# Loading the third dense stage's weights ahead of the query stores of the last layer

## The chip, the cores and the metric

The kernel runs on one core of one Trainium2 chip. The core has a matrix engine (PE, with its weight loads shown as PEld), a vector engine (DVE), an activation engine (ACT), a general engine (POOL) and SyncE (SP), which here only issues transfers. Transfers issued by SP and by POOL are carried out by the same 16 DMA engines. The metric is the time of one execution on the device in microseconds; lower is better. The instruction streams are written out by hand, and the engines meet only at semaphores.

## The reference

Four layers work on 8 sequences of 256 tokens with 256 features (2048 tokens). Each layer adds a gated cross-attention to a context and then a gated feed-forward stage. Cut to what matters:

```python
x = x + tanh(g_xattn[l]) * xattn_l(layernorm(x), ctx)   # 16 heads of 16
x = x + tanh(g_ffn[l]) * ffn_l(layernorm(x))
# ffn_0: light and heavy dense stage; ffn_1, ffn_2: 8 experts, top 2; ffn_3: ternary weights
def weight_quant(w):
    scale = 1.0 / clip(mean(abs(w)), 1e-05)
    return clip(round(w * scale), -1, 1) / scale
# ffn_3: h = bit_linear(x, w1); depthwise conv; silu; bit_linear(h, w2)
```

The weights of `ffn_3` are two matrices of 1024 x 256 floats, 1 MB each. `weight_quant` needs the mean absolute value of each whole matrix before any of it can be rounded.

## The kernel before

Attention keeps its operands as a high and a low part, each stored to memory and loaded again in a stacked form. For each of four groups of 512 tokens (g = 0 to 3), PE projects keys and values from the context, then queries from the normed and transposed x. ACT writes the high part (`keys` L1292, `queries` L1334), DVE the low part (`keys_low` L1764, `queries` L1774). SP stores both parts of a group to `qk_parts` in two transfers of 512 KB (`store_k` L397, `store_q` L404). POOL loads the stacks back for each sequence b (`load_stack` L547, rows of 1 KB), keys first, then queries, and waits for the stored group before each. A group's query parts sit in one of two buffers, so the high part of group 2 waits for the store of group 0, and that of group 3 for the store of group 1. The scores of the attention begin (`scores_nat` L849) when the low parts of all four groups are done and the stack of sequence 0 has landed.

The preceding stage, the experts of layer 2, ends with POOL gathering expert results by index from memory (L732, 32 transfers of 128 KB into `wslot`), and DVE adding them to `x_res` (L2150, four adds for each pair of token tiles, counted by `y_done[2]`). Between these adds DVE makes the low key parts of layer 3, so the projections of layer 3 start while the experts' results are still being added.

The ternary weights also go into `wslot`, into places that the first 24 adds have freed; hence the wait for `y_done[2]` at 24 in `load_ternary` (L411). Its two transfers, L414 (1 MB in rows of 4 KB) and L416 (1 MB in rows of 1 KB), count on `w0_in`. DVE sums the absolute values in `ternary_sums` (L1926, two reductions, L1928 and L1929), which it reaches after the low query part of group 1 and before those of groups 2 and 3. The rounding itself (L1909 to L1914) comes after the attention.

In layer 3, SP's stream is: the key stores of groups 0 to 3, the query stores of groups 0 and 1, the two weight loads, the query stores of groups 2 and 3, and nothing more until the output. SP takes them in this order and waits at each for its semaphores. Layer 2 has the same code for projections and stores without the ternary load; there POOL loads the first two experts (four transfers of 512 KB, L541 and L544) just ahead of its stack loads.

Of the kernel before, what the change touches and what calls it, by code (L numbers as in the profile page):

```python
# [95 lines left out]
def build(nc, io, upto=8):  # L96

    ctx = ExitStack()
    with ctx:
# [284 lines left out]
        @block.sync  # L384
        def _(sp):
            def load_ctx(g):
                sp.dma_start(ctx_at(g), io["ctxT"][:, g * 512:(g + 1) * 512].rearrange("(c p) t -> p c t", p=P)
                             ).then_inc(ctx_in[g], 16)
            for g in range(GROUPS):
                sp.dma_start(x_res[:, 4 * g:4 * g + 4, :],  # L390
                             io["x"][g * 512:(g + 1) * 512, :].rearrange("(t p) d -> p t d", p=P)).then_inc(x_in[g], 16)
                if g == 0:
                    sp.dma_start(ident[:], io["ident"]).then_inc(const_in, 16)
                    sp.dma_start(cols[:], io["cols"]).then_inc(const_in, 16)
                load_ctx(g)

            def store_k(l, g):  # L397

                sp.wait_ge(khi_done, GROUPS * l + g + 1)
                sp.wait_ge(klo_done, GROUPS * l + g + 1)  # L400
                for r, part in enumerate((k_hi(g), k_lo(g))):
                    sp.dma_start(rows_of(1, r, g), part.bitcast(F32)).then_inc(k_out[g % 2], 16)

            def store_q(l, g):  # L404

                sp.wait_ge(qhi_done, GROUPS * l + g + 1)
                sp.wait_ge(qlo_done, GROUPS * l + g + 1)
                for r, part in enumerate((q_hi(g), q_lo(g))):
                    sp.dma_start(rows_of(0, r, g), part.bitcast(F32)).then_inc(q_out[g % 2], 16)

            def load_ternary():  # L411

                sp.wait_ge(y_done[2], 24)
                sp.dma_start(wslot[:, 0, 0:2048].rearrange("p (c h) -> p c h", c=KC),  # L414
                             io["W1_3"].rearrange("(c p) h -> p c h", p=P)).then_inc(w0_in, 16)
                sp.dma_start(wslot[:, 1, 0:2048].rearrange("p (j d) -> p j d", d=D),  # L416
                             io["W2_3"].rearrange("(j p) d -> p j d", p=P)).then_inc(w0_in, 16)

            def load_proj(l):

                sp.wait_ge(xo_done[l - 1], B)
                sp.dma_start(wproj[:], io[f"wproj_{l}"].rearrange("w (c p) n -> p w c n", p=P)
                             ).then_inc(wproj_in, 16)
                sp.dma_start(bob[:], io[f"bo_{l}"]).then_inc(wproj_in, 16)

            for l in lo_l:
                if l in (1, 2):
                    if l == 2:
                        sp.wait_ge(lg_mm, GROUPS)
                    sp.dma_start(wg[:], io[f"wg_{l}"].rearrange("(c p) e -> p c e", p=P)).then_inc(wg_in, 16)  # L430
                if l == 0:

                    def load_mask(b):
                        for m, name in enumerate(("mask", "maskT")):
                            sp.dma_start(stage_i[:, b % 2, m].rearrange("p (a n) -> p a n", a=2),
                                         io[name][b * S:(b + 1) * S, :].rearrange("(a p) n -> p a n", p=P)
                                         ).then_inc(mask_in[b % 2], 16)
                    for b in range(2):
                        load_mask(b)
                if l == 0:  # L440
                    for g in range(GROUPS):
                        store_k(0, g)
                        store_q(0, g)
                        if g == 1:
                            sp.dma_start(v_in, io["ctx"].rearrange("(t p) d -> p t d", p=P)).then_inc(v0_in, 16)
                elif l == 1:
                    for g in range(GROUPS):
                        store_k(l, g)
                    for g in range(GROUPS):
                        store_q(l, g)  # L450
                else:
                    for g in range(GROUPS):
                        store_k(l, g)
                    for g in range(GROUPS):
                        if l == 3 and g == 2:
                            load_ternary()
                        store_q(l, g)
                if l == 0:
                    sp.dma_start(ys[2 * T:], io["ctx"][0:NT * P - 2 * T, :]).then_inc(later_in, 16)
                    sp.dma_start(tri[:], io["tri"]).then_inc(later_in, 16)  # L460
                    sp.dma_start(iotas[:], io["iotas"]).then_inc(later_in, 16)
                if l == 0:
                    for b in range(2, B):
                        sp.wait_ge(mask_done, b - 1)
                        load_mask(b)
                if l == 0:
                    sp.wait_ge(v_done, GROUPS)
                    sp.dma_start(wslots[:, 0:KC * NJ[0] * P].rearrange("p (c h) -> p c h", c=KC),
                                 io["W1_0"].rearrange("(c p) h -> p c h", p=P)).then_inc(w0_in, 16)
                    sp.wait_ge(sc_mm, 2 * PAIRS)  # L470
                    sp.dma_start(wslots[:, KC * NJ[0] * P:W0].rearrange("p (j d) -> p j d", d=D),
                                 io["W2_0"].rearrange("(j p) d -> p j d", p=P)).then_inc(w0_in, 16)
                if not ffn(l):
                    continue

                if l == 0:
                    sp.wait_ge(xo_done[0], B)
                    sp.dma_start(b2b[:], io["b2_0"]).then_inc(later_in, 16)
                    for g in range(GROUPS):
                        load_ctx(g)  # L480
                    load_proj(1)
                if l in (1, 2):
                    sp.wait_ge(xo_done[l], B)

                    for g in range(GROUPS):
                        sp.wait_ge(xn_ready, GROUPS * (2 * l + 1) + g + 1)
                        sp.dma_start(xt[g * 512:(g + 1) * 512, :].rearrange("(t p) d -> p t d", p=P), xn_slot(2 * l + 1, g)
                                     ).then_inc(xt_out, 16)
                    n0 = NT * (l - 1)

                    def load_tile(i, p):

                        sp.wait_ge(xg_mm, n0 + i - AHEAD + 1 if i < AHEAD + 2 else n0 + i - 1)
                        sp.dma_start(xg[:, p], home(i)).then_inc(xg_in[p], 16)

                    def store_tile(i, p):
                        sp.wait_ge(yo_done, n0 + i + 1)
                        sp.dma_start(ys[P * i:P * (i + 1), :], yo[:, p]).then_inc(ys_out[p], 16)
                    for i in range(AHEAD - 3):
                        store_tile(i, i % 2)  # L500
                    for i in range(AHEAD, NT):
                        if i in LATE:
                            n = LATE.index(i)
                            sp.wait_ge(late_in[n], 16 * (LATE[n + 1] - i) * l)
                        load_tile(i, i % 2)
                        if 0 <= i - 2 * AHEAD - 2 < GROUPS:
                            load_ctx(i - 2 * AHEAD - 2)
                        store_tile(i - 3, (i - 3) % 2)
                    load_proj(l + 1)
                    for i in range(NT - 3, NT):  # L510
                        store_tile(i, i % 2)

            if upto == 8:
                for g in range(GROUPS):
                    sp.wait_ge(y_done[3], 4 * (g + 1))
                    sp.dma_start(io["out"].rearrange("(t p) d -> p t d", p=P)[:, 4 * g:4 * g + 4, :],
                                 x_res[:, 4 * g:4 * g + 4, :]).then_inc(out_done, 16)
                sp.wait_ge(out_done, 16 * GROUPS)
            else:
                if upto % 2:  # L520
                    sp.wait_ge(xo_done[upto // 2], OUT[upto // 2])
                else:
                    sp.wait_ge(*ln_ready(upto // 2, upto))
                sp.dma_start(io["out"].rearrange("(t p) d -> p t d", p=P), x_res[:]).then_inc(out_done, 16)
                sp.wait_ge(out_done, 16)
# [1859 lines left out]
```

## Time and profile before

| | us |
|---|---|
| median of 3 runs | 1684.87 (1681.97 to 1688.16) |
| the profiled execution, its time | 1685.63 |
| its span in the trace | 1683.8 |
| busy: PE / DVE / ACT / POOL | 1358.9 / 999.3 / 825.0 / 652.9 |
| moved by DMA | 189.22 MB, 112 GB/s on average |

The span is what the trace covers; the profiled execution's own time is 1.83 us longer. Busy time is the time in which an engine executed instructions; a stretch in which every engine waits for a transfer does not show in it. The views used below are the chain of waits (the chain of work that ended last, followed back), the sums of waits by pair, the instructions in order of time, the issues of transfers with the time from issue to landing, and tables of stretches.

### The profile page before, as it was taken

To read this page: it belongs to the slowest core of one execution; us is meant where nothing else is said; L and a number is where in the kernel's file an instruction comes from. 1 tells how busy PE (TensorE), PEld (TensorE's weight loads), DVE (VectorE), ACT (ScalarE), POOL (GpSimd) and SP (SyncE) were. 2 spreads that over 40 slices of the span, in tenths; PEclk is the share of its full clock that TensorE was granted. 3 is DMA by queue.
4 is the path that set the end of the run, shared out by engine and by line. 5 is a ranking of instruction groups with operands and counts; after the bars stand their busy time and mean duration, and the time that the engine had idled before them with its cause. 6 is when DMAs were issued, how large, how long until landed. Compare 5 with 4: busy or idle time off the path is not lost.

```text
span 1683.8 us, 30045 instructions
## 1 busy us (share of the span) xinstructions
PE 1358.9 (81%) x9618; PEld 967.2 (57%) x9619; DVE 999.3 (59%) x2324; ACT 825.0 (49%) x1656; POOL 652.9 (39%) x711
## 2 busy tenths in 40 slices
PE   1399959998899659999998599658999837995875
PEld 1155528974565449999985355426777515564333
DVE  7266664342786753433336488684444628868787
ACT  2055545433588425555444388425555425872422
POOL 5363242011551058465216473008761626531000
PEclk9999978999799869999999799968999977997987
DMA  8997320028991325344125996114652597910001
GB/s 267 257 178 88 50 85 1 1 98 196 159 131 24 132 75 155 114 153 168 37 86 177 249 120 86 45 57 123 194 186 94 177 186 137 133 22 0 1 13 38
DMA packets 143757, 189.22 MB, mean 112 GB/s; under 512 B 21808, under 2 KB 110256, under 8 KB 143600
## 3 DMA queue, kind: packets, MB, share of 16 engines
q0 software_dynamic: 79264, 103.35, 33.8%
q1 hardware_dynamic: 64384, 84.41, 15.5%
q8 instruction: 68, 1.11, 0.3%
q14 instruction: 41, 0.34, 0.1%
HBM read 128.96 MB, written 50.99 MB: 107 GB/s over the span
## 4 chain that ended last, share of the span: by engine, by line
PE 59%; DVE 18%; DMA 9%; issue 4%; POOL 4%; ACT 4%; SPq 2%; ACTq 0%; DVEq 0%; POOLq 0%
PE PS L1073 10%; PE PS L1093 10%; PE PS L927 6%; PE PS L867 6%; PE PS L902 3%; PE PS L1085 3%; DMA stack<-mt 3%; DVE nm L1829 3%; PE PS L877 2%; DVE amx L2256 2%; DMA wslot<-ys_sorted,pos 2%; PE PS L910 2%; PE PS L964 1%; DVE xng L1713 1%; DMA wslot<-W_dram 1%
## 5 line engine op out<-in xcount | busy, mean ns | idle before, releaser
L1829 DVE TENSOR_REDUCE nm<-PS 128x2 f32<-128x512 f32 x512 | 336.4, 681 | 128.3 <-PE PS L867 51.6
L867 PE MATMUL PS<-stack 48*128 48x256 f32 x1024 | 141.0, 357 | 78.6 <-DVE nm L1829 26.2
L1093 PE MATMUL PS<-weights,hh 128*128 x936 | 187.5, 290 | 3.7 <-DVE hl L2108 3.5
L583 POOL DMA_DIRECT2D stack<-mt x128 | 71.3, 557 | 282.6 <-ACT mt L1402 280.3
L867 PEld LDWEIGHTS PS<-stack 48*128 48x128 f32 x1024 | 84.8, 204 | 164.0 <-DVE nm L1829 72.2
L1073 PE MATMUL PS<-weights,xh 128*128 x468 | 168.4, 414 | 11.8 <-ACT PS L1496 7.3
L1393 ACT ACTIVATE probs<-PS 128x512 f32<-128x512 f32 x256 | 139.0, 595 | 58.6 <-PE PS L910 31.0
L1393 ACT ACTIVATE xng<-PS 128x512 f32<-128x512 f32 x256 | 138.9, 595 | 46.9 <-PE PS L910 28.3
L1093 PEld LDWEIGHTS PS<-weights,hh 128*128 128x128 f32 x936 | 150.8, 191 | 7.7 <-issue 6.4
L1093 PE MATMUL PS<-weights,hl 128*128 x468 | 132.4, 283 | 0.0
L1506 ACT ACTIVATE hh<-PS 128x512 fp32r<-128x512 f32 x117 | 65.7, 596 | 134.5 <-PE PS L1085 134.5
L902 PE MATMUL PS<-stack 49*128 49x256 f32 x1024 | 113.3, 299 | 8.0 <-DMA stack<-mt 5.1
L1073 PEld LDWEIGHTS PS<-weights,xh 128*128 128x128 f32 x468 | 89.4, 191 | 38.2 <-issue 20.7
L1496 ACT ACTIVATE PS<-bb 128x512 f32 x117 | 67.2, 596 | 63.3 <-issue 61.6
L753 PE MATMUL PS<-ident,xng 128*128 128x128 f32 x192 | 34.5, 344 | 77.4 <-DVE xng L1713 58.8
L902 PEld LDWEIGHTS PS<-stack 49*128 49x128 f32 x1024 | 84.4, 196 | 18.2 <-issue 10.2
L1073 PE MATMUL PS<-weights,xl 128*128 x234 | 92.8, 396 | 0.0
L562 POOL DMA_DIRECT2D stack<-qk_parts x128 | 68.4, 534 | 58.7 <-DMA qk_parts<-q_parts 45.0
L1093 PEld LDWEIGHTS PS<-weights,hl 128*128 128x128 f32 x468 | 89.7, 192 | 0.0
L681 POOL TENSOR_TENSOR weights<-weights,zero 128x4096 fp32r<-128x4096 f32 (+1 forms) x12 | 63.8, 5315 | 50.5 <-DMA weights<-W_dram 50.4
L684 POOL TENSOR_TENSOR weights<-weights 128x4096 fp32r<-128x4096 f32 (+1 forms) x12 | 81.8, 6820 | 1.0
L2108 DVE TENSOR_TENSOR hl<-PS,hh 128x512 fp32r<-128x512 f32 x117 | 76.8, 684 | 6.3 <-ACT hh L1506 6.1
(298 smaller groups left out, 3039.9 us busy)
## 6 DMA issues: line engine op xcount, KB each, us to landing
stack<-qk_parts POOLq DMA_DIRECT2D x128, 256.0 KB, 4.3
qk_parts<-stack SPq DMA_DIRECT2D x32, 512.0 KB, 4.6
qk_parts<-q_parts SPq DMA_DIRECT2D x32, 512.0 KB, 6.9
stack<-qk_parts POOLq DMA_DIRECT2D x128, 128.0 KB, 3.7
weights<-W_dram POOLq DMA_DIRECT2D x12, 1024.0 KB, 7.7
ys_sorted<-yo SPq DMA_DIRECT2D x78, 128.0 KB
wide<-ctxT_dram SPq DMA_DIRECT2D x16, 512.0 KB, 7.6
weights<-W_dram POOLq DMA_DIRECT2D x12, 512.0 KB, 5.3
```

Source lines behind the costliest of these rows:

```text
L562: nc.gpsimd.dma_start(rows(first, 1), part[0:DH]).then_inc(stack_in[b % SLOTS], 16)
L583: nc.gpsimd.dma_start(stack[MAXROW:MAXROW + 65:64, b % SLOTS, 0, c:c + 2, :].rearrange("p c n -> p (c n)"), mt[:, j % 4, :]).then_inc(row_ ...
L684: nc.gpsimd.tensor_tensor(wl, w, wh.bitcast(F32), ALU.subtract).then_inc(split_done, 1)
L867: mm = pe.matmul(PS[:, (2 * t + h) % 3, qt * S:(qt + 1) * S], q[rows, qt * P:(qt + 1) * P], kk[rows], start=(l > 0 or qt == 0), stop=(l > ...
L902: mm = pe.matmul(PS[:, 3 + (2 * t + h) % 3, kt * S:(kt + 1) * S], kk[rows, kt * P:(kt + 1) * P], q[rows], start=(l > 0 or kt == 0), stop=( ...
L927: mm = pe.matmul(PS[32 * strip:32 * strip + 32, 6, 0:S], vpad[:, 2 * b + kt, (DH + 1) * head:(DH + 1) * head + 32], probs_at(t, h)[:, kt * ...
L1073: add = lambda x, w: pe.matmul(PS[:, hid_bank(p) + h, :], x[:, p, c, :], w, start=False, stop=True, skip_group_check=True)
L1093: add = lambda x, w: pe.matmul(o, x, w, start=False, stop=True, skip_group_check=True)
L1393: nc.scalar.activation(probs_at(t, h), PS[:, 3 + (2 * t + h) % 3, :], ACT.Exp, scale=SCALE).then_inc(exp_done, 1)
L1496: nc.scalar.activation(PS[:, hid_bank(p) + h, :], bb[:, ds(off + (D + h * 512), 512)], ACT.Identity).then_inc(pre_done, 1)
L1829: nc.vector.tensor_reduce(nm[:, j % 2, at:at + 2], PS[:, (2 * t + h) % 3, :].rearrange("p (q n) -> p q n", q=2), AX.X, ALU.max, negate=Tru ...
L2108: nc.vector.tensor_tensor(hl[:, at].rearrange("p j t -> p (j t)"), PS[:, 3 + h, :], hh[:, at].rearrange("p j t -> p (j t)").bitcast(F32), ...
```

## The change

SP issues the two weight loads after the four key stores and ahead of all query stores of layer 3, in place of between the stores of groups 1 and 2. Their own wait, their sizes and their places are as before.

```diff
                     for g in range(GROUPS):
                         store_k(l, g)
+                    if l == 3:
+                        load_ternary()
                     for g in range(GROUPS):
-                        if l == 3 and g == 2:
-                            load_ternary()
                         store_q(l, g)
```

SP's stream in layer 3 before, from the key store of group 2 on (`stack` is where the key parts are kept, `q_parts` where the query parts are):

```order
L402 DMA qk_parts<-stack 128x2x512 [waits klo_done,khi_done]
L402 DMA qk_parts<-stack 128x2x512
L402 DMA qk_parts<-stack 128x2x512 [waits klo_done,khi_done]
L402 DMA qk_parts<-stack 128x2x512
L409 DMA qk_parts<-q_parts 128x2x512 [waits qlo_done,qhi_done]
L409 DMA qk_parts<-q_parts 128x2x512
L409 DMA qk_parts<-q_parts 128x2x512 [waits qlo_done,qhi_done]
L409 DMA qk_parts<-q_parts 128x2x512
L414 DMA wslot<-W_3_dram 128x2x1024 [waits y_done2]
L416 DMA wslot<-W_3_dram 128x8x256
L409 DMA qk_parts<-q_parts 128x2x512 [waits qlo_done,qhi_done]
L409 DMA qk_parts<-q_parts 128x2x512
```

The same place in SP's stream now:

```order
L402 DMA qk_parts<-stack 128x2x512 [waits klo_done,khi_done]
L402 DMA qk_parts<-stack 128x2x512
L402 DMA qk_parts<-stack 128x2x512 [waits klo_done,khi_done]
L402 DMA qk_parts<-stack 128x2x512
L414 DMA wslot<-W_3_dram 128x2x1024 [waits y_done2]
L416 DMA wslot<-W_3_dram 128x8x256
L409 DMA qk_parts<-q_parts 128x2x512 [waits qlo_done,qhi_done]
L409 DMA qk_parts<-q_parts 128x2x512
L409 DMA qk_parts<-q_parts 128x2x512 [waits qlo_done,qhi_done]
L409 DMA qk_parts<-q_parts 128x2x512
L409 DMA qk_parts<-q_parts 128x2x512 [waits qlo_done,qhi_done]
L409 DMA qk_parts<-q_parts 128x2x512
```

The two loads have moved ahead of four query store transfers; the wait for `y_done[2]` has moved with them and now stands ahead of the first query store.

DVE's stream is the same before and now; this is where it meets the loads:

```order
L1784 SCALAR_TENSOR_TENSOR q_parts<-PS,cols,q_parts 128x512 [waits q_out1,qhi_done,ln_v6]
L1784 SCALAR_TENSOR_TENSOR q_parts<-PS,cols,q_parts 128x512
L1928 TENSOR_REDUCE q<-wslot 128x1 [waits w0_in]
L1929 TENSOR_REDUCE q<-wslot 128x1
L1784 SCALAR_TENSOR_TENSOR q_parts<-PS,cols,q_parts 128x512 [waits q_out0,qhi_done]
L1784 SCALAR_TENSOR_TENSOR q_parts<-PS,cols,q_parts 128x512
```

The reductions, with the wait for both loads, stand between the low query parts of group 1 and group 2. The streams of PE, ACT and POOL are the same too.

## Rows read from the trace of the kernel before

**Rows 1.** Chain of waits, 1345 to 1393 us: start, length, what.
```profile
1345.83 5.70 DMA wslot<-ys_sorted,pos
...
1351.55 0.48 DVE x_res L2150
...
1361.60 0.47 SPq L409
...
1363.04 22.08 DMA wslot<-W_dram
...
1387.35 2.28 DVE q L1929
1389.62 2.64 DVE q_parts L1784 x4
```

**Rows 2.** Waits by pair, 1330 to 1420 us: total, times, longest.
```profile
DVE q L1928 <- DMA wslot<-W_dram: 24.0, 1, 24.0
...
PE PS L867 <- DVE q_parts L1784: 23.2, 1, 23.2
```

**Rows 3.** SP in order of time: start, us, line, what.
```profile
1315.52 30.00 SPq L402 DMA_DIRECT2D qk_parts<-stack  x8
1355.37 6.71 SPq L409 DMA_DIRECT2D qk_parts<-q_parts  x4
1362.12 0.88 SPq L414 DMA_DIRECT2D wslot<-W_dram  x1
1363.04 1.39 SPq L416 DMA_DIRECT2D wslot<-W_dram  x1
```

**Rows 4.** DVE in order of time, around the last adds of layer 2.
```profile
1340.04 1.28 DVE L2150 SCALAR_TENSOR_TENSOR x_res<-wslot,gt,x_res 128x256 f32<-128x256 f32 x3 [3.92 <-DMA wslot<-ys_sorted,pos]
...
1345.68 2.07 DVE L2150 SCALAR_TENSOR_TENSOR x_res<-wslot,gt,x_res 128x256 f32<-128x256 f32 x5
...
1359.72 1.41 DVE L1784 SCALAR_TENSOR_TENSOR q_parts<-PS,cols,q_parts 128x512 fp32r<-128x512 f32 x2 [3.34 <-ACT q_parts L1339]
```

**Rows 5.** ACT in order of time, high query parts of groups 2 and 3.
```profile
1361.51 1.26 ACT L1339 ACTIVATE q_parts<-PS,cols 128x512 fp32r<-128x512 f32 x2 [1.88 <-DMA qk_parts<-q_parts]
...
1369.13 1.26 ACT L1339 ACTIVATE q_parts<-PS,cols 128x512 fp32r<-128x512 f32 x2 [5.38 <-PE PS L794]
```

**Rows 6.** PE in order of time, layer 3, last projection and first scores.
```profile
1363.80 5.29 PE L794 MATMUL PS<-wide,wproj 128*128 128x512 f32 x8 [3.81 <-ACT wide L1331]
1392.31 0.80 PE L867 MATMUL PS<-stack 48*128 48x256 f32 x4 [23.22 <-DVE q_parts L1784]
```

**Rows 7.** Transfers issued 1363.25 to 1363.6: size, us to landing.
```profile
wslot<-W_dram SPq DMA_DIRECT2D x1, 1024.0 KB, 22.1
stack<-qk_parts POOLq DMA_DIRECT2D x1, 256.0 KB, 14.2
```

**Rows 8.** Chain of waits, layer 2, 926 to 949 us.
```profile
927.34 10.15 DMA qk_parts<-q_parts
...
939.70 5.73 PE PS L794 x8
```

**Rows 9.** Layer 2 in order of time: ACT, high query part of group 3; PE, first scores.
```profile
945.45 1.09 ACT L1339 ACTIVATE q_parts<-PS 128x512 fp32r<-128x512 f32 x2 [5.81 <-PE PS L794]
...
947.91 0.50 PE L867 MATMUL PS<-stack 48*128 48x256 f32 x4 [2.50 <-DVE q_parts L1784]
```

**Rows 10.** POOL in order of time, layer 2, first expert load.
```profile
924.03 0.75 POOL L541 DMA_DIRECT2D wslot<-W_dram  x1 [4.33 <-DVE x_res L2150]
```

**Rows 11.** Transfers issued 926.9 to 927.6.
```profile
qk_parts<-q_parts SPq DMA_DIRECT2D x2, 512.0 KB, 9.2
wslot<-W_dram POOLq DMA_DIRECT2D x1, 512.0 KB, 8.0
```

**Rows 12.** PE, transposes of the attention's output, layers 2 and 3: ns, first and last start.
```profile
L951 PE MATMUL PS<-ident,wide x32: 272/273/273, 1064.7 to 1079.0; 128*128 128x128 f32 x32
...
L951 PE MATMUL PS<-ident,wide x32: 272/273/273, 1506.8 to 1523.2; 128*128 128x128 f32 x32
```

**Rows 13.** Query store L409, all 32 transfers: us to landing.
```profile
DMA to landing us min/median/max: 2.8/6.9/17.2
```

**Rows 14.** Stretches: us, busy and count by engine, PEclk, DMA share, GB/s.
```profile
1345.00:1350.00 5.00, 2.29 (x18) 1.74 (x16) 2.61 (x9) 4.32 (x9) 4.69 (x9) 1.00 0.91 291
1350.00:1355.00 5.00, 5.00 (x8) 1.98 (x8) 4.26 (x14) 1.04 (x3) 0.52 (x1) 0.66 1.51 152
...
1361.10:1385.14 24.04, 5.29 (x8) 2.09 (x8) 0.03 (x1) 3.50 (x6) 5.99 (x11) 0.69 1.23 213
...
1405.00:1410.00 5.00, 5.00 (x37) 3.06 (x39) 3.02 (x5) 3.27 (x8) 3.41 (x7) 0.50 0.57 82
```

**Rows 15.** Transfers issued 1355.3 to 1356.
```profile
qk_parts<-q_parts SPq DMA_DIRECT2D x2, 512.0 KB, 4.8
```

## Prediction, made before the changed kernel ran

> **What bounds the kernel now.** I read the order of instructions first, then the chain of waits around the moved transfers, because the change touches nothing else. The chain's longest single piece there is a transfer: the second weight load holds it for 22.08 us from its issue at 1363.04 [rows 1]. The sums of waits show two sides of it: DVE stands 24.0 us at its first reduction, and PE stands 23.2 us ahead of the first scores, released by DVE's low query parts [rows 2]. So the stall is not hidden: DVE cannot make the low parts of groups 2 and 3 until the weights are summed, and the scores want all four. The stream of SP tells why the loads come late: it issued its last key store before 1345.52 (1315.52 + 30.00), then waited until 1355.37 for the low query part of group 0, and only after the stores of groups 0 and 1 the loads, at 1362.12 and 1363.04 [rows 3].
>
> Before 1361 the chain runs through the last gather (1345.83, landing after 5.70 us), the last add at 1351.55, and the low parts of groups 0 and 1 [rows 1]. DVE is then ready for the sums at 1359.72 + 1.41 = 1361.1 [rows 4].
>
> **What is removed.** The wait on `y_done[2]` costs SP nothing in its new place. The last eight of the 32 adds are those that begin at 1345.68; the 24th is the last of the three that begin at 1340.04 and is over by 1341.3 [rows 4], and SP is there at 1345.5. The loads then issue at about 1345.5 and 1346.4 (L414 took 0.88 us) and SP is free at 1347.8 (1.39 us more [rows 3]), 7.5 us before the first query store is ready. The loads are issued 16.6 us earlier.
>
> With the wait for weights gone, the next thing in line is the high query part of group 3. ACT started group 2 at 1361.51, released by the store of group 0, and group 3 at 1369.13, after PE's cold projection of 5.29 us [rows 5, 6]. How long from there to the first scores? Layer 2 has the same code and no ternary sums: ACT began group 3 at 945.45 and PE its scores at 947.91, 2.46 us later [rows 9]. Added to 1369.13 this gives 1371.6. DVE has room for the sums, about 4.5 us (1389.62 - 1385.14, both reductions, by the end of the wait [rows 1]) between 1361.1 and 1370.4; a low part takes 1.4 us [rows 4], and 1361.1 + 4.5 + 1.4 = 1367.0. The scores began at 1392.31 [rows 6], so the largest gain is 1392.3 - 1371.6 = 20.7 us. For all of this to be hidden, the weights may land as late as about 1364.5 (1370.4 - 4.5 - 1.4); every us later costs one.
>
> When do they land? Before, it took 22.1 us for the second load, beside two further megabytes of stack loads and stores, at 213 GB/s [rows 7, 14]: so 1368.5 at the latest. From the other side, layer 2 issued four loads of 512 KB from 924.03 on, and the last landed 8.0 us after its issue near 926.3, about 10.2 us for 2 MB with a query store and the key stacks beside it [rows 10, 11]: 1355.7. The new place has the last key store, the last gathers and 768 KB of key stacks beside it, so it is nearer to layer 2. I take 1359, and the term is nothing; both ends stay in the range.
>
> **What is added.** Three tolls, all by sharing the DMA engines.
>
> First, the last gather. It is on the chain and is in flight (1345.83 to 1351.53) exactly when the loads now start. The stretch from 1345 moved 291 GB/s without them [rows 14]. By its size, 128 KB beside 1 MB in long rows, and the slow case (the stack load of 14.2 us beside the ternary load, twice the gather's size [rows 7]), the bounds are 0 and about 7 us; I take 1.5, since most of the gather's time lies in the first 3 us.
>
> Second, the query store of group 0. It releases ACT's group 2 and POOL's query stacks, and on SP's queue it now stands behind the 2 MB. It took about 5.7 us from its second issue (1355.8 to 1361.51), the pair 4.8 us in the middle [rows 5, 15]. In layer 2 the same store, issued within a microsecond of the last expert load, took 10.15 us [rows 8], 4.5 us more. Here it follows the loads by some nine microseconds, so I take 1.5 of these 4.5. The low end is 0; the high end is the second load's old 22.1 us in full, after which the store takes its 5.7: 1368.5 + 5.7 = 1374.2 in place of 1361.5, or 12.7.
>
> The Trainium skill, "DMA: Bandwidth & Descriptors", section on queues, rings and completion order, says that each DMA engine consumes one queue's descriptors in ring order and takes turns between queues. By that rule the store cannot start before the weights' descriptors are consumed, which is the high end if the load is as slow as before and nothing if it is over by 1357. No row shows a store behind a load on one queue. The same page's fit (section on the anatomy of one DMA) of 2.0 us plus bytes over 436 GB/s would give 6.8 us for 2 MB, an estimate by that page, and so no toll here; the trace's 22.1 us for half of it disagrees.
>
> Third, the start of the attention. In layer 3 the queues had run empty during the stall. In layer 2 they had not, and from the first scores to the first output transpose it took 1064.7 - 947.91 = 116.8 us against 1506.8 - 1392.31 = 114.5 us [rows 6, 9, 12]. I charge this 2.3 us. It may be nothing, or even a gain: after the long idle PE still ran at the granted clock of 0.50, the lower of its two levels, until 1410 [rows 14], and four score matmuls took 0.80 us in place of 0.50 [rows 6, 9]. Some 11 such steps at 0.3 us would be 3.3 us, the other end of this term.
>
> All later work hangs on the scores and nothing in it waits on the loader, so the shift should carry to the end.
>
> **The sum.** 20.7 - 1.5 - 1.5 - 2.3 = 15.4 us. The scores begin at 1371.6 + 3.0 = 1374.6, and the profiled execution's 1685.63 becomes 1670.2. It was 0.8 above the median of 1684.87, so I say 1670.
>
> **The rivals.**
>
> *The load is as slow as before and the store waits behind it.* The ordering speaks for it. Store lands at 1374.2, plus 10.1 us to the first scores (1371.6 - 1361.5) gives 1384.3: 8.0 us gained, 2.3 given back, 1679.9. Against it: the megabytes beside the load are fewer, and from 1350 to 1355 only 152 GB/s moved [rows 14].
>
> *The query stacks of sequence 0 become the last thing.* Before, they had 14.2 us from the last issue [rows 7] but were covered by the stall. With the store at 1364.5, the last stack load issues 1.8 us later (1363.3 against 1361.5) and lands at 1380.5: gain 11.8 - 2.3 = 9.5, 1676.1. Against it: the slow landing was itself beside the ternary load.
>
> *No tolls.* The gain is 20.7 us, or up to 24.0 with a warm PE: 1664.9 to 1661.6. For it: the DMA engines had room.
>
> *Slower.* One mechanism: the backlog on SP's queue makes the stores late, and the stack loads behind them late too. With weights at 1368.5, the store of group 0 taking the longest of all 32, 17.2 us [rows 13], and the last stack load 1.8 us after it taking 14.2 us, the stacks are there at 1401.7, 9.4 us after the old start: 1695.0. It decides once the store lands after about 1376.3 by way of the stacks, or 1382.2 by way of ACT. For it: the store and the stack loads do queue so. Against it: each had these landings under more traffic than will be here.
>
> *The change doesn't do what it says* would need SP to be held by the adds; the four microseconds between 1341.3 and 1345.5 speak against, and I give it no chance of its own.
>
> **How the numbers follow.** Forecast (gain of 10 to 20 us, 1665 to 1676) 0.60; no tolls 0.14; stacks last 0.08; slow load and late store 0.13; slower 0.05. Within 0.5% (8.4 us, about what a measurement of this kernel can tell from no change) lies the slow load alone; faster are the first three, 0.82. The range takes in the warm end, 1662, and the slow load, 1681.
>
> **What the changed profile would show.** Right: L414 issued near 1345.5; DVE waits for the weights at L1928 for at most a microsecond or two; PE's idle before the first scores of layer 3 is some 4 to 6 us in place of 23.2, and what releases it is still L1784, now behind ACT's group 3; the scores begin near 1374.6. The last gather's landing over 5.70 us sizes the first toll, the first L409 of layer 3 the second, the stretch from scores to output transposes, 116.8 against 114.5, the third. Wrong: DVE still waits over 8 us at L1928, or the store of group 0 lands after 1372, or PE waits for the stack.

## The result, and the profile after

| | before | after |
|---|---|---|
| median of 4 runs, us | 1683.42 (1681.52 to 1688.16) | 1669.47 (1667.37 to 1675.03) |
| ratio, 95% interval | | 0.9916 (0.9895 to 0.9937) |
| profiled execution, us | 1685.63 | 1675.03 |
| its span, us | 1683.8 | 1673.2 |

By the ratio the kernel became 0.84% faster, 14.1 us of 1683.4; 1670 had been forecast. The profiled execution was the slowest of the four of the changed kernel, so its trace holds 10.6 us of the gain.

First the chain of waits of the changed kernel over the place of [rows 1].

```profile
1348.61 10.12 DMA wslot<-ys_sorted,pos
...
1358.75 0.48 DVE x_res L2150
...
1362.97 5.95 DMA qk_parts<-q_parts
...
1370.80 9.45 DMA stack<-qk_parts
...
1380.48 0.81 PE PS L867 x4
...
1385.40 5.46 DMA stack<-mt
```

No weight load is on it. Two other transfers stand there now: the last gather, 10.12 us in place of 5.70 (these are the chain's steps, from issue to the add's start), and a query stack load of 9.45 us, which ends just ahead of the first scores.

The waits by pair, as [rows 2], say the same: there is no row for L1928, and PE's wait ahead of the scores is 5.5 us, for a stack and not for DVE.

```profile
PE PS L867 <- DMA stack<-qk_parts: 5.5, 1, 5.5
```

SP in order of time, as [rows 3].

```profile
1318.61 28.83 SPq L402 DMA_DIRECT2D qk_parts<-stack  x8
1347.49 0.92 SPq L414 DMA_DIRECT2D wslot<-W_dram  x1
1348.45 1.45 SPq L416 DMA_DIRECT2D wslot<-W_dram  x1
1362.57 16.13 SPq L409 DMA_DIRECT2D qk_parts<-q_parts  x8
```

The loads go out directly after the last key store (1318.61 + 28.83 = 1347.44), with no wait for the adds. The whole stage began 3.1 us later in this execution than in that of before (1318.61 against 1315.52), so only stretches are compared below, not clock times.

DVE and ACT in order of time, as [rows 4, 5].

```profile
1355.15 0.88 DVE L2150 SCALAR_TENSOR_TENSOR x_res<-wslot,gt,x_res 128x256 f32<-128x256 f32 x2 [5.48 <-DMA wslot<-ys_sorted,pos]
1358.75 0.48 DVE L2150 SCALAR_TENSOR_TENSOR x_res<-wslot,gt,x_res 128x256 f32<-128x256 f32 x1 [2.72 <-DMA wslot<-ys_sorted,pos]
...
1361.08 1.41 DVE L1784 SCALAR_TENSOR_TENSOR q_parts<-PS,cols,q_parts 128x512 fp32r<-128x512 f32 x2
...
1368.24 2.28 DVE L1928 TENSOR_REDUCE q<-wslot 128x1 f32<-128x2048 f32 x1
1370.43 2.27 DVE L1929 TENSOR_REDUCE q<-wslot 128x1 f32<-128x2048 f32 x1
```

```profile
1369.00 1.26 ACT L1339 ACTIVATE q_parts<-PS,cols 128x512 fp32r<-128x512 f32 x2 [2.18 <-DMA qk_parts<-q_parts]
...
1375.03 1.26 ACT L1339 ACTIVATE q_parts<-PS,cols 128x512 fp32r<-128x512 f32 x2 [3.79 <-PE PS L794]
```

The sums start without a wait. What has grown is the wait for the gathers, 5.48 and 2.72 us before the last three adds (before: 2.75 and 0.18).

To set the executions side by side I cut the transition into three stretches. A: from the last gather's issue to the low query part of group 0 (L1784), which holds the gather's landing. B: from there to the first scores, which held the wait for the weights. C: from the first scores to the first output transpose, the attention. Before, by [rows 1, 6, 12] and the low part's start at 1353.88: A 8.1, B 38.4, C 114.5. After: 1361.08 - 1348.61 = 12.5, 1380.48 - 1361.08 = 19.4, 1498.7 - 1380.48 = 118.2, the last by this row, as [rows 12].

```profile
L951 PE MATMUL PS<-ident,wide x32: 272/273/273, 1498.7 to 1515.1; 128*128 128x128 f32 x32
```

### The profile page after: what moved, and what is told of

The parts are those of the page before. It is cut to its first block, busy times and chain, and to the rows that moved or that the text cites. A ratio compares the mean times of both kernels' runs of the same rounds, so it can differ in the third digit from the quotient of the medians.

```text
span 1673.2 us, 30018 instructions
## 1 busy us (share of the span) xinstructions
PE 1355.0 (81%) x9591; PEld 965.9 (58%) x9619; DVE 998.5 (60%) x2324; ACT 824.9 (49%) x1656; POOL 652.7 (39%) x711
## 3 DMA queue, kind: packets, MB, share of 16 engines
q1 hardware_dynamic: 64384, 84.41, 15.5%
## 4 chain that ended last, share of the span: by engine, by line
PE 60%; DVE 17%; DMA 9%; issue 5%; ACT 4%; POOL 3%; SPq 1%; ACTq 1%; DVEq 0%; another core or an unknown queue 0%; POOLq 0%
PE PS L1073 10%; PE PS L1093 10%; PE PS L927 7%; PE PS L867 6%; PE PS L902 3%; DMA stack<-mt 3%; PE PS L1085 3%; DVE nm L1829 3%; PE PS L877 2%; DMA wslot<-ys_sorted,pos 2%; DVE amx L2256 2%; PE PS L910 2%; PE PS L964 1%; DVE xng L1713 1%; PE PS L768 1%
## 5 line engine op out<-in xcount | busy, mean ns | idle before, releaser
L1073 PE MATMUL PS<-weights,xh 128*128 x468 | 168.2, 414 | 12.5 <-ACT PS L1496 7.2
L1073 PEld LDWEIGHTS PS<-weights,xh 128*128 128x128 f32 x468 | 89.3, 191 | 38.8 <-issue 21.4
L753 PE MATMUL PS<-ident,xng 128*128 128x128 f32 x192 | 34.2, 341 | 75.8 <-DVE xng L1713 58.3
```

The costliest lines, as they stand in the source:

```text
L1073: add = lambda x, w: pe.matmul(PS[:, hid_bank(p) + h, :], x[:, p, c, :], w, start=False, stop=True, skip_group_check=True)
```

## The experiments

Twelve kernels ran, in three sets of four (e1 to e4, e5 to e8, e9 to e12), each set on another chip. Ratios are to the kernel before in the same set. A, B and C come from each kernel's own trace, in us.

| | ratio (95%) | A | B | C |
|---|---|---|---|---|
| before, first trace | | 8.1 | 38.4 | 114.5 |
| after, first trace | 0.9916 (0.9895 to 0.9937) | 12.5 | 19.4 | 118.2 |
| e1 small loads | 0.9875 (0.9829 to 0.9921) | - | 17.3 | 116.0 |
| e2 wait for 32 adds | 0.9911 (0.9884 to 0.9937) | - | 20.0 | 116.2 |
| e3 between stores | 0.9907 (0.988 to 0.9934) | - | 23.1 | 118.1 |
| e4 sums late | 0.9941 (0.992 to 0.9961) | - | 18.7 | 116.3 |
| e5 before again | 1.0026 (1.0004 to 1.0048) | 8.7 | 35.7 | 114.9 |
| e6 after again | 0.9923 (0.9896 to 0.995) | 11.9 | 17.9 | 117.3 |
| e7 small loads again | 0.9932 (0.9907 to 0.9957) | 9.0 | 18.8 | 116.7 |
| e8 wait for 32 again | 0.9932 (0.9909 to 0.9955) | 8.0 | 22.8 | 113.8 |
| e9 double | 0.9967 (0.9949 to 0.9986) | 12.4 | 23.6 | 116.2 |
| e10 split | 0.994 (0.9918 to 0.9963) | 14.8 | 19.1 | 118.4 |
| e11 after | 0.9929 (0.9903 to 0.9954) | 10.6 | 18.8 | 116.0 |
| e12 wait for 32 | 0.9926 (0.9901 to 0.9951) | 7.1 | 21.4 | 116.4 |

Two limits of the table. The kernel before measured 0.26% against itself (e5), so ratios that differ by less than about 0.003 are not told apart. And in the first set the kernels took some 1750 to 1770 us (before 1771.76). The traces show a part of what was longer: among other such waits, ACT stood for 16 to 18 us at L1309, released by a queue that the profile does not name, ahead of the last adds of layer 2. The row is from the waits of e2.

```profile
ACT vpad L1309 <- remote: 16.0, 1, 16.0
```

DVE then made its last eight adds without a wait for a gather, so A says nothing there. The changed kernel itself was not in that set.

**e1 and e7, the loads cut to a sixteenth.**

```diff
-sp.dma_start(wslot[:, 0, 0:2048].rearrange(...), io["W1_3"].rearrange(...))
+sp.dma_start(wslot[:, 0, 0:128], io["W1_3"][0:P, 0:128])
-sp.dma_start(wslot[:, 1, 0:2048].rearrange(...), io["W2_3"].rearrange(...))
+sp.dma_start(wslot[:, 1, 0:128], io["W2_3"][0:P, 0:128])
```

> The changed kernel with each weight load cut from 1 MB to 64 KB, at the new place (it leaves out the rest of the ternary weights, so the last dense stage works on other data; its instructions are the same). Theory: the changed kernel loses part of its gain to the two megabytes that now share the DMA engines with the last gather and the stacks. Then the last gather lands in about 5.7 us in place of 10.1, the last query stack of sequence 0 in about 7 in place of 9.5, the first scores come 26 to 28 us after the last gather's issue (changed kernel 31.9), and the time is about 1665. Rival: the slower gather is an accident of that one execution or of something else in the new order. Then the gather stays near 10 us and the time near 1669.

> The changed kernel with each weight load cut from 1 MB to 64 KB (the last dense stage then works on other data, its instructions are the same). Theory: gather at 5 to 6.5 us, first scores 15 to 18 us after the first query store's issue, ratio to before 0.986 to 0.989, so 4 to 6 us better than the changed kernel. Rival: the toll is chance, and the two are within 1.5 us.

In the first set this was the best kernel (0.9875, with an interval that overlaps those of e2 and e3), in the second no better than the changed one (0.9932 against 0.9923). The traces are clearer. A fell from 11.9 to 9.0 against e6 in the same set, and the gather's step of the chain in e7, 9.51 us in e6, was this:

```profile
1348.39 6.64 DMA wslot<-ys_sorted,pos
```

So the bytes of the loads do hold up the last gather. But B did not fall, 18.8 against 17.9: in e7 it was the store of group 1 that came late, 8.22 us, issued just behind the stack loads of group 0 and without any weights in flight. In the changed kernel, where the store of group 0 landed later, it went out just ahead of them (4.90 us). The expected 4 to 6 us over the changed kernel were not there in the times: by them the rival, that the two are within 1.5 us, came true. So the traces show that the bytes hold up the gather, but no measured time shows what taking them away would be worth.

**e2, e8 and e12, the loads after the last add.**

```diff
-                sp.wait_ge(y_done[2], 24)
+                sp.wait_ge(y_done[2], 32)
```

> The changed kernel, but the loads wait for all 32 adds of layer 2 and not for 24, so they start after the last gather has landed and still ahead of the query stores. Theory of shared engines: the gather is back at 5.7 us, the weights land some 10 to 12 us after their issue, DVE waits 0 to 3 us at its sums, the first query store lands in 8 to 10 us in place of 5.95, and the first scores come 29 to 32 us after the last gather's issue; time 1667 to 1670, no slower than the changed kernel. Rival, load time as in the kernel before (22.1 us): DVE waits some 13 us and the scores come at 41 us, time 1678.

> The loads of the changed kernel held back until all 32 adds of layer 2 are done. Theory: the last gather is back at 5 to 6.5 us where ACT does not stand; in exchange the first query store lands 7 to 8 us after its issue (7.7 in the first call) and not 6, so the first scores come 17 to 20 us after its issue, and the time is 0 to 3 us better than the changed kernel. Rival: the store behind the loads costs all that the gather gains, and more; then the time is 2 to 5 us worse.

> The loads held back until all 32 adds are done. Theory: last gather 5.5 to 6.5 us, first query store 8 to 9 us, first scores 30 to 31 us after the gather's issue as in the changed kernel, and a quicker start of the attention (113.8 us to the output transposes in its first trace, against 117.3 and 118.2), so 1 to 3 us better than the changed kernel: ratio 0.990 to 0.992. Rival: that quicker start was chance, and the two are equal.

The chain of waits of e8:

```profile
1346.83 5.66 DMA wslot<-ys_sorted,pos
...
1356.74 8.92 DMA qk_parts<-q_parts
...
1368.03 6.77 PE PS L794 x8
```

The gather is back at 5.66 us, and the first query store, which now follows the loads by three microseconds, takes 8.92 in place of 5.58 (e6) and 5.95. A falls by 3.9 (e8 against e6) and 3.5 (e12 against e11), B rises by 4.9 and 2.6. The quicker attention of e8 (113.8) was not seen again in e12 (116.4). The times are equal: 0.9926 beside 0.9929 in one set; the expected 1 to 3 us of e12 did not come.

The rise of B has two parts. The store is some 3 us later. And ACT's group 3 waits longer for PE's last projection, which took 6.77 us in e8 and 5.31 in e12; in the traces of the changed kernel it took 3.70. These stretches are that projection in the changed kernel and in e8:

```profile
1371.30:1375.00 3.70, 3.70 (x8) 1.43 (x8) 2.72 (x3) 0.00 (x0) 3.69 (x8) 1.00 1.19 214
1368.03:1374.79 6.76, 6.76 (x8) 2.50 (x8) 0.93 (x2) 0.00 (x0) 3.90 (x8) 0.54 1.65 212
```

The granted clock (third number from the end) was 1.00 and 0.54, so most of e8's projection ran at the lower level. PE had stood 7.08 us just before it, behind the late store, and 2.05 us in the changed kernel. Against both parts, the wait for the stack ahead of the scores is gone (1.9 us in e6, 2.0 in e11). So both traces show that the loads hold up whichever transfer of the chain is next to them; that this costs the same at either place is a sum of unlike parts.

**e3, the loads one store later.**

```diff
-                        if l == 3 and g == 2:
+                        if l == 3 and g == 1:
                             load_ternary()
```

This is against the kernel before.

> The loads stand between the query stores of groups 0 and 1, one store later than in the changed kernel and one earlier than before. Theory of shared engines: gather 5.7 us, first query store about 6, weights land 12 to 16 us after issue at about 1356.3 of the old clock, DVE waits 7 to 11 us, and the stack loads of sequence 0 run beside the weights and take 10 to 14 us; first scores 33 to 37 us after the last gather's issue (before 46.5, changed 31.9), time 1671 to 1676. Rival, each place later costs its full issue delay: the scores come 11 us after those of the changed kernel, at 42, time 1679.

DVE in order of time, around the sums of e3:

```profile
1459.49 2.29 DVE L1928 TENSOR_REDUCE q<-wslot 128x1 f32<-128x2048 f32 x1 [8.46 <-DMA wslot<-W_dram]
```

DVE waits 8.46 us, as expected (7 to 11), and B is 23.1, 3 us more than e2's. The place between the two orders gives a wait between 0 and 24 us. But this wait did not set B by itself: the chain of waits of e3 runs through the store of group 1, which was issued behind the 2 MB.

```profile
1451.52 12.52 DMA qk_parts<-q_parts
```

It landed at 1464.04 and released ACT's group 3; DVE's sums were over at the same time (1461.69 + 2.27 = 1463.96). The time, 0.9907, is not told apart from e2's 0.9911.

**e4, the loads left where they were and DVE's sums moved behind the attention.**

```diff
-                if l == 2 and ffn(3):
-                    ternary_sums()
...
+                    if l == 3 and ffn(3):
+                        ternary_sums()
                     add_out(l, ternary() if l == 3 and ffn(3) else [])
```

> The loads stay where they were in the kernel before; DVE sums the weights after the attention and not between the query parts. So the wait for the weights is gone without moving a transfer. Theory: with DVE free, the query stacks of sequence 0 become the last thing, since they still load beside the 2 MB (14.2 us, there at 1377.5): first scores 31 to 33 us after the last gather's issue, as in the changed kernel, gather at 5.7 us, 4.5 us of sums added behind the attention; time 1672 to 1675. Rival: the scores are held by ACT and PE only, and come 25.8 us after the gather; time 1667.

No transfer was moved ahead of another, and B fell to 18.7 all the same. So the 17 to 20 us that B is longer in the kernel before (38.4 and 35.7, traces of other sets) were DVE standing in its own order for the weights; the late landing itself, 19.26 us for L416 in e4, held up nothing ahead of the scores once DVE did not wait for it there. What I had expected to come last, the stacks, did not: DVE's low part of group 3 released PE, after ACT had waited for the store of group 1.

```profile
1464.50 0.80 PE L867 MATMUL PS<-stack 48*128 48x256 f32 x4 [5.04 <-DVE q_parts L1784]
```

The sums themselves, free in the changed kernel, are now on the chain behind the attention, 4.48 us, and the ratio is 0.9941. In e4's chain of waits:

```profile
1581.43 2.27 DVE q L1928
1583.70 2.21 DVE q L1929
```

**e5, e6 and e11, the two kernels again.**

> The kernel before, profiled on the chip of this call, as the base for the others. In the first call ACT stood 16 to 18 us at one instruction for a queue that the profile does not name, just ahead of the last adds of layer 2, and all kernels there were some 5% slower. Theory: the effect of the change does not hang on that; from the first query store's issue to the first scores it takes 36 to 38 us, as in the first trace of before (36.9), with DVE waiting about 24 us for the weights. Rival: the wait for the weights is shorter where ACT stands, since the loads find emptier queues, and the change is worth less there.

> The changed kernel on the same chip. Theory: no wait for the weights, first scores 17 to 20 us after the first query store's issue (17.9 in its first trace), last thing a query stack of sequence 0 or ACT's group 3; ratio to before 0.989 to 0.993. If ACT does not stand here, the last gather again takes 9 to 10.5 us; if it does, the gathers are early and this toll does not show. Rival: the toll at the gathers is chance; then it is under 7 us where ACT does not stand.

> The changed kernel again, beside the others of this call. Theory: ratio 0.991 to 0.993, gather 9 to 10.5 us, first scores 30 to 32 us after it. Rival: none of its own; it sizes the scatter between executions.

B of before was 38.4 and 35.7, with DVE waiting 24.02 and 21.32 us; of the changed kernel 19.4, 17.9 and 18.8. A rose from 8.1 and 8.7 to 12.5, 11.9 and 10.6. The ratios fell in the expected ranges, but some spans did not: 34.2 us from the first query store to the scores in e5 (36 to 38 expected), 16.4 in e6 (17 to 20), and in e11 the last two gathers took 8.93 and 8.15 us (9 to 10.5) and the scores came 29.4 us after the last one's issue (30 to 32). In all three traces of the changed kernel the last thing before the scores is a query stack; this is e6:

```profile
1378.37 0.50 PE L867 MATMUL PS<-stack 48*128 48x256 f32 x4 [4.38 <-DMA stack<-qk_parts]
```

**e9, two more megabytes behind the loads.**

```diff
+                sp.dma_start(xt[0:1024, :], io["W1_3"].rearrange("a (b d) -> (a b) d", d=D)).then_inc(extra, 16)
+                sp.dma_start(xt[1024:2048, :], io["W2_3"]).then_inc(extra, 16)
```

> The changed kernel with two more megabytes behind the two weight loads, a copy of the same weights from memory to a place in memory that nothing reads any more, at the same point of SP's queue. Theory: what the new place costs is the bytes beside the last gather and ahead of the query store, so doubling them doubles the toll and brings the store's in: last gather 11 to 15 us (changed kernel 9.5 to 10.1), first query store 8 to 14 us (5.6 to 6), first scores 36 to 42 us after the last gather's issue (29.8 to 31.9); ratio to before 0.995 to 1.000, so most of the gain is gone. Rival: the queues have room, and the ratio stays within 0.003 of the changed kernel's 0.992.

More than half of the gain is gone, 0.9967, in the middle of what was expected. The gather was expected at 11 to 15 us, and that missed. By the trace, the extra bytes did not touch it, only what came after it:

```profile
1345.35 10.04 DMA wslot<-ys_sorted,pos
...
1359.64 9.88 DMA qk_parts<-q_parts
...
1371.90 6.70 PE PS L798 x8
```

A is 12.4, no more than in the changed kernel: the gather lands while the first megabytes are still under way. The first query store behind them takes 9.88 us (6.11 in e11), and the projection after it, L798 in this kernel, 6.70 in place of 3.70, at a granted clock of 0.55 after PE had stood 5.58 us. B rises to 23.6.

**e10, the first load ahead already between the key stores.**

```diff
-            def load_ternary():
...
-                sp.wait_ge(y_done[2], 24)
+            def load_first():
...
+                sp.wait_ge(y_done[2], 8)
...
+            def load_second():
...
+                sp.wait_ge(y_done[2], 24)
...
                     for g in range(GROUPS):
+                        if l == 3 and g == 2:
+                            load_first()
                         store_k(l, g)
                     if l == 3:
-                        load_ternary()
+                        load_second()
```

> The first weight load goes ahead already after the key store of group 1, as soon as 8 adds are done and its place is free; the second stays at the changed kernel's place. Theory: 1 MB less beside the last gather, which comes back to 7 to 8.5 us, but an earlier gather is held up by 1 to 3 us while the first load runs; first scores 28 to 30 us after the last gather's issue; in the sum 0 to 2 us better than the changed kernel. Rival: earlier gathers have slack, POOL's issuing being the limit there, and all of 3 us is won.

This missed. The earlier gather was held up: 8.58 us in e10's chain of waits, where before had 4.39 at that place in e5. But the last gather was not relieved:

```profile
1327.56 8.58 DMA wslot<-ys_sorted,pos
...
1351.37 12.41 DMA wslot<-ys_sorted,pos
```

It took 12.41 us with 1 MB beside it, more than with 2 MB (8.15 to 10.12) or 4 MB (10.04), each in one to three traces. So the toll did not go with the number of bytes issued. In e10 the load beside the gather is the one in rows of 1 KB; in the others the one in rows of 4 KB goes first. Whether that is the reason was not tried. The time, 0.994, is not told apart from the changed kernel's 0.9929.

## Why the prediction was right

**The stall and its removal.** Right. The weights' wait at L1928 is gone, SP was not held by the adds, and B of the changed kernel was to be 38.4 - 20.7 + 1.5 = 19.2 us by the terms of the prediction; it was 19.4, 17.9 and 18.8. e4 shows by another way that the long B was DVE's wait. That 19.2 and 19.4 lie so close is luck: by its pieces, B of the first trace had 1.2 us less than forecast up to ACT's group 2 (7.9, not 9.1), 1.6 us less from there to ACT's group 3 (6.0, not 7.6), and 3.0 us more from there to the scores. The middle piece was overlooked. The prediction kept PE's projection at 5.29 us, as in this stretch of before with a granted clock of 0.69; in all three traces of the changed kernel it took 3.70 us at 1.00.

```profile
1363.80:1369.09 5.29, 5.29 (x8) 2.08 (x8) 0.00 (x0) 0.00 (x0) 3.89 (x8) 0.69 1.06 206
```

**The weights' landing.** The term was right, its ground was not. I took 1359, some 13.5 us after the first issue. It was 1348.45 + 18.0 = 1366.5 by the landing of L416, 19 us after the first issue, nearer to the old 22.1 than to layer 2's 10. It cost nothing because the prediction's own margin was wide enough: on the clock of before it landed at 1363.4 (1366.5 - 3.1), and up to 1364.5 had been worked out as free. That DVE did not wait at all is due to the late gather, which had moved its sums to 1368.24. The second load of e8, issued when the gathers were through, took 9.7 us to land; this is the same count in the changed kernel.

```profile
DMA to landing us min/median/max: 18.0/18.0/18.0
```

**First toll, the gather: mis-sized.** Forecast 1.5 us; by A it was 4.4 in the first pair of traces, 3.2 in the second set (11.9 - 8.7), and against the mean of before 2.2 in e11. I had argued that most of the gather's time lies in its first 3 us; but its whole flight lay inside that of the first load (1347.49 to 1359.67), and two gathers are out at once. The bounds held it.

**Second toll, the store behind the loads: not settled.** Forecast 1.5 on a base of 5.7; the first query store took 5.95, 5.58 and 6.11 us. In the first pair of traces that is 0.3 more than before. But the base itself is not firm: the same store took 3.75 us in e5, the kernel before again, and 3.74 in e7, without the bytes, so in the second set the toll was 1.8. With it the first two tolls are 4.7 and 5.0 us in the two sets, where 3.0 had been forecast. e8 and e9 show that the store's toll grows when it follows closely or more stands ahead of it, 8.92 and 9.88 us.

The ring-order rule that the prediction takes from the Trainium skill ("DMA: Bandwidth & Descriptors", section on queues, rings and completion order) fits e9: the store issued behind 4 MB on its queue was 4 us late. Sharing of the engines alone could look the same, and no run here tells the two apart. The fit in the same page of the Trainium skill, 6.8 us for 2 MB, is given there for transfers issued from GpSimd; here the two loads, issued by SP beside other traffic, took 19 us, and 10.1 us in e8.

**The stacks.** Missed: PE waits for the stack, which the prediction had named as a sign of being wrong. I gave it as a rival that the query stack becomes last; it did in all three traces, but by little: 2.46 us after ACT's group 3 the scores could have begun, at 1377.5, and they began at 1380.48, 3.0 us later (1.9 in e6, 2.0 in e11). The rival's price assumed a 14.2 us landing and that was 9.45.

**Third toll, the attention's start.** Forecast 2.3; 118.2, 117.3 and 116.0 against 114.5 and 114.9 make 2.5 on the mean. In this stretch the query stacks of sequence 1 are still under way, which before had landed during the stall, and the query stores of groups 2 and 3 land 11.3 to 13.1 us after their issue (2.8 to 5.1 before, where they were issued only as the scores began). That this is the cause is not shown. The granted clock is a rival: over the first 60 us of C it was 0.84 and 0.85 before and 0.80, 0.80 and 0.84 in the changed kernel, it was lowest in e10 and e3 (0.76 and 0.77), where C was 118.4 and 118.1, and highest in e8 (0.86), where C was 113.8.

**The sum.** The means of A + B + C are 160.2 us before (161.0, 159.3) and 147.5 after (150.1, 147.1, 145.4): 12.6 us, against 15.4 forecast and 14.1, 12.9 and 12.0 by the three ratios. In the first pair, 15.4 less 2.9 for the gather, 3.0 for the stacks and 1.4 for the attention, and plus 1.2 for the store and 1.6 for the projection, is the 10.9 that the traces show. The timed gain is 3 us more, 14.1, the profiled execution being the slowest of four. So the errors of the terms partly cancelled and scatter did the rest: that 1670 was met within 1 us is in part luck. What makes the executions of one kernel differ by several microseconds no run here resolves.

**Slower.** The mechanism exists, as e9 shows, but 4 MB in place of 2 only brought the ratio to 0.9967.

## What to carry to other kernels

An engine that waits in program order for data needed much later stalls all that is queued behind it; look for it where one engine's wait equals another's, and fix the order of either side: the load (0.992) or, if the work behind is short, the consumer (0.994). When a bulk load is moved forward, name the transfer on the chain that will be in flight beside it: by the traces, 2 MB made the last gather 2 to 4 us longer, or the next store 3 us. Shifting the load by a few microseconds between the two won nothing that the times show. And look at what a later transfer does to PE: in e8 and e9 the wait behind the late store was followed by a projection at the lower clock, which cost about as much again.

## What the runs showed that I had not expected

The toll on a 128 KB gather did not grow with what was issued beside it: 10.12, 9.51 and 8.15 us with 2 MB, 10.04 with 4 MB, 12.41 with 1 MB in rows of 1 KB, against 5.70 and 6.31 without. And the second 1 MB load took 18.0, 17.1 or 17.0 us when issued beside the last gathers and 9.7 or 9.8 when issued 6 to 7 us later (e8, e12; counted, as what follows, from the last gather's issue). The later ones had landed after 16.3 us (1353.44 + 9.7 - 1346.83) and 15.5, the earlier ones after 17.9 (1366.5 - 1348.61), 16.8 and 16.2: holding the load back did not make it late.
